# Where and when the turned query weights are loaded, and the weight folding one feed-forward tile earlier, in a two-layer decoder

## The reference

```
h   = sigmoid(xq @ Wg) * (xq @ Wu)      # xq: x rounded to 8 bits by row, W: ternary
x   = layernorm(x + quant(h) @ Wd)             # feed-forward, d_ff = 1024

c   = x @ Wkvc                                 # latent, 64 wide, shared by all heads
k_h = [c @ Wkdec_g, rope(c @ Wkrope_g)]        # 4 key groups g for 16 heads h
q_h = [x @ Wq_h,    rope(x @ Wqrope_h)]
x   = layernorm(x + softmax(causal(q k^T)) v @ Wo),   v = c @ Wvdec_g
```

## Time and profile before

| what | value |
|---|---|
| median of 3 runs (lowest to highest) | 765.69 us (765.66 to 766.63) |
| the profiled execution: its time | 770.09 us |
| its span | 767.6 us |
| mean granted TensorE clock | 0.942 |
| TensorE busy, of the span | 654.6 us, 85% |
| VectorE, ScalarE, GpSimd busy | 63%, 57%, 26% |
| moved by DMA | 62.02 MB, mean 81 GB/s |

### The profile page before, as it was taken

How to read it: one execution, slowest core, us unless ns; L and a number is a source line. 1 busy time by engine, 2 the same in 40 slices (tenths; PEclk the granted TensorE clock), 3 DMA queues, 4 the chain that set the end, 5 groups by cost and what they waited for, 6 DMA issues and landing times.

```text
span 767.6 us, 13772 instructions
## 1 busy us (share of the span) xinstructions
PE 654.6 (85%) x4748; PEld 531.9 (69%) x4749; DVE 483.6 (63%) x1091; ACT 436.3 (57%) x1123; POOL 201.2 (26%) x364
## 2 busy tenths in 40 slices
PE   6788787998999998878978999999986299999950
PEld 4566577998988988843545677777776178778840
DVE  1577776577586577475845656566557567777735
ACT  3988846457456456446866646464523256566622
POOL 2455510040010010011213334252326402223224
PEclk9999999999999999987999999999999589999985
DMA  8995000220220220043020000000078211111114
GB/s 303 378 321 165 1 1 1 86 87 1 88 86 1 86 87 1 1 194 81 1 83 1 1 1 3 1 1 2 1 304 327 68 30 48 48 55 48 48 46 145
DMA packets 31921, 62.02 MB, mean 81 GB/s; under 512 B 2452, under 2 KB 26776, under 8 KB 29624
## 3 DMA queue, kind: packets, MB, share of 16 engines
q1 hardware_dynamic: 29848, 56.04, 21.7%
q0 software_dynamic: 2016, 5.22, 1.9%
HBM read 45.80 MB, written 15.55 MB: 80 GB/s over the span
## 4 chain that ended last, share of the span: by engine, by line
PE 57%; ACT 19%; DVE 15%; issue 4%; POOL 3%; DMA 2%; SPq 0%; POOLq 0%; ACTq 0%; DVEq 0%
PE banks L1726 34%; PE bank L1726 23%; ACT arena L742 5%; DVE U_split L1205 4%; ACT arena L1010 4%; ACT U_split L761 2%; DVE mx L1159 1%; DVE dmx L1487 1%; ACT arena L1017 1%; POOL rstd L550 1%; POOL xs L646 1%; DMA ys<-arena 1%; ACT arena L780 1%; DVE arena L1444 1%; DVE bmx L1224 1%
## 5 line engine op out<-in xcount | busy, mean ns | idle before, releaser
L1726 PE MATMUL banks<-U_split 128*128 128x512 f32 (+1 forms) x616 | 147.8, 352 | 4.7 <-DVE U_split L1205 1.9
L1726 PE MATMUL bank<-U_split 128*128 128x256 f32 (+1 forms) x864 | 115.6, 290 | 15.3 <-DVE U_split L1205 15.2
L1726 PEld LDWEIGHTS bank<-U_split 128*128 128x128 f32 x864 | 108.6, 194 | 19.6 <-issue 15.0
L1726 PEld LDWEIGHTS banks<-U_split 128*128 128x128 f32 x616 | 97.0, 190 | 26.6 <-issue 11.6
L761 ACT ACTIVATE U_split<-arena 128x1024 fp32r (+6 forms) x122 | 97.2, 821 | 14.0 <-issue 5.3
L1726 PE MATMUL banks<-cst,arena 128*128 128x128 f32 (+1 forms) x594 | 83.7, 277 | 14.0 <-DMA arena<-xs 11.1
L1726 PE MATMUL banks<-arena 128*128 (+4 forms) x632 | 84.8, 382 | 8.3 <-ACT arena L1010 5.0
L547 POOL TENSOR_SCALAR rstd<-mv 128x1 f32<-128x1 f32 x48 | 11.8, 245 | 301.4 <-DVE mv L1137 269.5
L1726 PEld LDWEIGHTS banks<-cst,arena 128*128 128x128 f32 (+1 forms) x594 | 68.7, 142 | 24.0 <-issue 13.6
L1010 ACT ACTIVATE arena<-banks,dmx 128x128 f32<-128x128 f32 (+1 forms) x128 | 52.1, 419 | 53.8 <-DVE dmx L1487 53.8
L623 POOL TENSOR_SCALAR arena<-arena,dri 128x128 f32<-128x128 f32 (+1 forms) x128 | 52.6, 429 | 91.9 <-DVE dri L1455 91.9
(11 more groups left out here) (225 smaller groups left out, 1161.6 us busy)
## 6 DMA issues: line engine op xcount, KB each, us to landing
arena<-in_w_exp SPq DMA_DIRECT2D x8, 1536.0 KB, 14.3
xs<-arena SPq DMA_DIRECT2D x8, 1032.0 KB, 14.1
arena<-in_ctxT SPq DMA_DIRECT2D x4, 1601.0 KB, 7.2
arena<-in_ctx SPq DMA_DIRECT2D x4, 1536.0 KB
arena<-in_w_f SPq DMA_DIRECT2D x3, 1024.0 KB, 11.6
arena<-xs SPq DMA_DIRECT2D x23, 129.0 KB, 2.0
w_x<-in_w_x SPq DMA_DIRECT2D x9, 256.0 KB, 7.3
arena<-in_w_oh SPq DMA_DIRECT2D x1, 2048.0 KB, 8.1
```

What stands on the lines that cost most here:

```text
L1726: return nc.tensor.matmul(o, w, x, start=start, stop=stop, **k)
```

## The change

- `w_qT` is cut in two (heads 0 to 11 at the start of `ctxT[LO]`'s place, heads 12 to 15 at the start of `ctxT[HI]`'s), `w_qrT` in three (heads 0 to 7 behind the second part of `w_qT`, heads 8 to 11 and 12 to 15 in the places of the row images). `w_qe`, `w_mapT`, `w_vo` and `w_vh` move.
- SyncE loads both parts of `w_qT` and the first of `w_qrT` after the last scores and the last key products, ahead of its wait for `w_oh`'s place. The other two parts are loaded where all was loaded before; they have a semaphore of their own, waited for ahead of `d_fold(4)`. `d_fold(0)` now counts four loads.
- `d_fold(0)` moves from step 2 of the tile loop, behind `f_gate_up(3)`, to step 1, ahead of `f_hiddenT(0)`. Every later fold and turn-back moves up one tile. The last step has no fold, and the turn-back of pair 7 stands at its head, no longer behind `d_query(0)`. ScalarE's order follows.

The matmuls and their operands are the same.

```diff
+        CUT_Q, CUT_R = 12, (8, 12)
+        w_qT_0 = U1.cut(CUT_Q, E)
...
+        w_qT_1 = U1.cut(H1 - CUT_Q, E)
+        w_qrT_0 = U1.cut(CUT_R[0], E)[0:RD, :, :]
...
+            sp.wait_ge(G["b_s"], 4 * TPB * B)
+            sp.wait_ge(G["x_k"], CP * B)
+            load(w_qT_0, d["w_qT"][:, 0:CUT_Q, :], "ld_wqo")
+            load(w_qT_1, d["w_qT"][:, CUT_Q:H1, :], "ld_wqo")
+            load(w_qrT_0, d["w_qrT"][:, 0:CUT_R[0], :], "ld_wqo")
             sp.wait_ge(G["w_tern"], 3)
             load(w_oh, d["w_oh"], "ld_wqo")
             sp.wait_ge(G["b_o"], 2 * B)
-            load(w_qT, d["w_qT"], "ld_wqo")
-            load(w_qrT, d["w_qrT"], "ld_wqo")
+            load(w_qrT_1, d["w_qrT"][:, CUT_R[0]:CUT_R[1], :], "ld_wqr")
+            load(w_qrT_2, d["w_qrT"][:, CUT_R[1]:H1, :], "ld_wqr")
...
 def d_fold(t):
-                    pe.wait_ge(G["ld_wqo"], 48)
+                    pe.wait_ge(G["ld_wqo"], 64)
...
+                if 2 * t == CUT_R[0]:
+                    pe.wait_ge(G["ld_wqr"], 32)
...
 for t in range(NT + 1):
-                if t >= 3:
-                    d_turn_back(t - 3 if t < NT else t - 2)
+                if t >= 2:
+                    d_turn_back(t - 2 if t < NT else t - 1)
+                if t == 1:
+                    d_fold(0)
                 if t > 0:
                     f_hiddenT(t - 1)
                 if t + 1 < NT:
                     f_gate_up(t + 1)
-                if t > 1:
-                    d_fold(t - 2 if t < NT else t - 1)
+                if 1 < t < NT:
+                    d_fold(t - 1)
                 if t > 0:
                     f_down(t - 1)
                 if t == NT - 1:
-                    d_turn_back(t - 2)
+                    d_turn_back(t - 1)
...
                 if t == NT - 1:
-                    d_fold(t - 1)
+                    d_fold(t)
...
             d_query(0)
-            d_turn_back(NT - 1)
             d_latent(0)
```

More of the change, by code:

```diff
@@ L237, in build, with w_qT, w_qrT @@
         zeros = U1.cut(E + 2)
+        CUT_Q, CUT_R = 12, (8, 12)
         U1.start(0)
+        w_qT_0 = U1.cut(CUT_Q, E)
+        U1.start(CT_W)
         w_qe = U1.cut(KT, H1, LAT)
+        w_mapT = U1.cut(E)
+        w_qrT_1 = U1.cut(CUT_R[1] - CUT_R[0], E)[0:RD, :, :]
+        assert U1.at <= SLOT
+        U1.start(SLOT)
+        w_qT_1 = U1.cut(H1 - CUT_Q, E)
+        w_qrT_0 = U1.cut(CUT_R[0], E)[0:RD, :, :]
+        assert U1.at <= SLOT + CT_W
+        U1.start(SLOT + CT_W)
         w_vo = U1.cut(PAIRS, E)
[L241 to L244, removed]
+        w_qrT_2 = U1.cut(H1 - CUT_R[1], E)[0:RD, :, :]
+        U1.start(0)
         w_vh = U1.cut(PAIRS, E)
+        def w_qT(h):
+            return w_qT_0[:, h, :] if h < CUT_Q else w_qT_1[:, h - CUT_Q, :]
+        def w_qrT(h):
+            if h < CUT_R[0]:
+                return w_qrT_0[:, h, :]
+            return w_qrT_1[:, h - CUT_R[0], :] if h < CUT_R[1] else w_qrT_2[:, h - CUT_R[1], :]
         w_f32 = U2.cut(3, 2 * FF)
@@ L353, in build @@
         eri = sb("eri", [P, TPB, KT * HT])
-        names = """ld_x ld_q0 ld_k0 ld_v0 ld_rows ld_x01 ld_ctxT ld_ctxR ld_ffn_lat ld_cbias ld_wqo ld_out
+        names = """ld_x ld_q0 ld_k0 ld_v0 ld_rows ld_x01 ld_ctxT ld_ctxR ld_ffn_lat ld_cbias ld_wqo ld_wqr ld_out
             const_set ln_var ln_rstd ln_done xT_raw xT_done
@@ L928, in _ @@
             for t in range(NT + 1):
-                if t >= 3:
-                    d_turned_back(t - 3 if t < NT else t - 2)
+                if t >= 2:
+                    d_turned_back(t - 2 if t < NT else t - 1)
+                if t == 1:
+                    d_folded(0)
                 if t > 0:
@@ L951, in _ @@
                     d_split_w(1)
-                if t > 1:
-                    d_folded(t - 2 if t < NT else t - 1)
+                if 1 < t < NT:
+                    d_folded(t - 1)
                 if t == NT - 1:
-                    d_turned_back(t - 2)
+                    d_turned_back(t - 1)
                 if t % TPB == 0 and t // TPB + 1 < B:
@@ L960, in _ @@
                 if t == NT - 1:
-                    d_folded(t - 1)
-            d_turned_back(NT - 1)
+                    d_folded(t)
             d_latent(0)
@@ L2135, in d_fold @@
                 for i in range(2):
-                    mm(half(i, 0), w_kd[:, g, :], w_qT[:, 2 * t + i, :], stop=False)
+                    mm(half(i, 0), w_kd[:, g, :], w_qT(2 * t + i), stop=False)
                 for i in range(2):
-                    mm(half(i, 0), k_turn[:, 2 * t + i, :], w_qrT[:, 2 * t + i, :], start=False)
+                    mm(half(i, 0), k_turn[:, 2 * t + i, :], w_qrT(2 * t + i), start=False)
                 for i in range(2):
```

## The result

The changed kernel takes 773.81 us (median of four runs, 769.81 to 776.51) against 765.74 for the kernel before (four runs): a ratio of 1.0091, 95% interval 1.0054 to 1.0129. Run again with many more runs of both, it is 1.0057, 1.0032 to 1.0082. The forecast was 763.6 us with a range up to 767.0. The change makes the kernel slower, by 0.6 to 0.9%.

What follows compares the result with a forecast made beforehand. TensorE, with 57% of the chain, bounds the kernel; a 2.15 us stall before `d_fold(0)` and the low clock behind it were the target. 1.2 us at tile 3 plus 0.9 in the tail, off 765.69: 763.6 us, range 762.0 to 767.0.

Steps and rivals of the forecast that it cites:

- Early loads: `w_qT` and first `w_qrT` part, issued after the last scores, land by 324 and cost nothing; `w_oh` still issued at 335.07.
- The fold doesn't fill the gap: TensorE's 3.92 us gap before `f_hiddenT(0)`: `d_fold(0)` still waits for `w_oh`, landing at 343.2 after 8.1 us (7.5 to 9.5).
- `w_oh` lands sooner: Rival, chance 0.11: without the loads behind it `w_oh` lands near 342.0, the fold mostly fills the gap; 762.3 us.
- Cost at the start: `d_fold(0)` at low clock delays `f_hiddenT(0)` by 3.8 us; with 1.0 to 1.3 regained in `f_gate_up(2)`, tile 1 comes 2.8 late.
- the clock comes back late: Rival, chance 0.26: the rise at 347.9 moves behind `f_gate_up(2)`, 1.4 us more, 765.0 us, no visible change.
- What comes back: Between tiles 2 and 3, 4.27 us of stall and low-clock work vanish; less 2.8 and 0.3, tile 3 comes 1.2 us earlier.
- the sum: Whole kernel: 1.2 us from tile 3 plus 0.9 in the tail, 2.1 us gained, taken off the median 765.69: 763.6 us.
- The tail: After tile 7, `d_latent(0)` follows `d_query(0)` at once, without a turn-back between: 0.9 us gained.
- slower rival: Rival, chance 0.15: a clock fall behind the wait before `f_down(6)` costs up to 3.4 us, 767.0; 0.11 ends slower.
- the rest moves as a block: Behind the feed-forward stage, from the latent attention on, all shifts together and changes no length.
- The level: Profiled execution 770.09 us, median 765.69, 4.4 us lower; the gain was taken off the median though its clock history may differ.
- the fall behind the stall: TensorE around `d_fold(0)`: a 2.15 us stall near 352, followed by 6.8 us at half clock, 354.7 to 361.5.

Runs made afterwards that it cites:

- c_after: The changed kernel again, unchanged, in the same batch as c_before: 773.18 us, ratio 1.0057 to the kernel before.
- e1: The changed kernel's early loads and new places, with folds and turn-backs in the order of the kernel before: 767.35 us, ratio 0.9991 to the kernel before.
- e7: The changed kernel with the two late `w_qrT` loads issued only after `w_oh` has landed: ratio 1.0055 to the kernel before.
- e9: The changed kernel with first fold behind `f_gate_up(2)`, late `w_qrT` loads after `w_oh`'s landing, idle matmuls in the tail's waits: 765.09 us, ratio 0.9948 to before.
- e10: e9 without the idle matmuls in the tail: ratio 0.9988 to the kernel before.
- c_before: The kernel before again, unchanged: 768.07 us, ratio 1.0011.
- c_before2: The kernel before once more, unchanged, one profiled execution: 761.26 us.
- e8: The changed kernel with 27 idle matmuls in three waits of the feed-forward stage's tail: ratio 1.0023 to the kernel before.
- e2: The changed kernel with the first fold behind `f_gate_up(2)`, not ahead of `f_hiddenT(0)`: 767.37 us, ratio 0.9988 to the kernel before.
- e6: The changed kernel with 40 idle matmuls ahead of `d_fold(0)` while TensorE waits for `w_oh`: 770.78 us, ratio 1.0041 to the kernel before.
- e4: The changed kernel whose first fold multiplies query weights in place of `w_oh`, so doesn't wait for it: 769.55 us, ratio 1.0005 to the kernel before.

## Why the prediction was wrong

**Early loads: right.** Issued at 310, landed in time, `w_oh` issued as before (335.15 in c_after, 335.07 in the earlier trace rows). e1 shows that nothing is lost by them.

**The fold doesn't fill the gap: right, and mis-sized.** It waited for `w_oh` and ran at the low clock with groups 1.05 us apart. But the landing took 8.8 and 9.5 us; I took 8.1, the row of before, and 9.5 was my upper end. With two small loads onto 64 partitions behind it, `w_oh` takes longer (8.7 to 10.3 us in the kernels that have them there, 7.7 to 8.1 before, 8.2, 7.9 and 8.1 in e7, e9 and e10). In these three nothing is queued behind it, in the kernel before two large loads are, and the landing is the same: my rival "`w_oh` lands sooner" had the wrong premise. The Trainium skill's fit ("DMA: Bandwidth & Descriptors", "Anatomy of one DMA") gave 6.8; no landing of `w_oh` here is that short.

**"Cost at the start", 2.8 us: it was 4.1 and 5.2 to 5.4.** Of the excess 0.7 to 1.4 us is the landing. The rest is the clock: I gave back 1.0 to 1.3 us because `f_gate_up(2)` would fall behind the rise at 347.9. Counted from the issue of `w_oh` that is 12.8 us; the rise came at 14.7 in the profile shown of after, amid these matmuls, and at 16.1 in c_after, behind nearly all of them. 0.4 and 0.1 us came back. That was my rival "the clock comes back late": it came in half in one profile, in full in the other.

**"What comes back", 4.27 us: the step that failed.** I read the 9.91 us between tiles 2 and 3 of before as a property of the kernel. It differs from execution to execution. Without the fall, seen in c_before and c_before2, the distance is 6.8 and 6.2 us, and the kernel after has 5.9: 0.3 to 0.9 us come back, not 4.0. Against the one profile that I had read, the term did come out, at 4.0; there the 5.8 us that the forecast missed are 1.3 at the start, 3.4 in the tail and 1.1 behind it. But the sum was taken off the median of other, faster runs. From tile 3 to tile 7 both take 22.2 to 22.3 us, so the shift is kept, as forecast; only it is +3.6 to +4.6 us and not -1.2.

**The tail, -0.9 us: not seen.** `d_latent(0)` did follow `d_query(0)` at once, and the gain went into the clock: tile 7 to the first score takes 15.3 and 13.8 us, where before has 12.8, 14.3 and 14.0. This is the mechanism of my slower rival, and its place was right: behind the wait of 1.96 us ahead of `f_down(6)`. A second wait, 1.12 us ahead of the last `f_down`, is new: `d_fold(7)` had stood there, and I had costed its leaving at nothing, "as the queries wait for VectorE". A step that hides nothing may still keep the clock up: in all nine profiles of the new order of folds without idle matmuls in the tail the clock is low behind this wait or the next, ahead of `d_query(0)`, in none of the five of the old order (e1 is the fifth) and in neither of e8 and e9, where the waits are filled. But against the usual 14.0 to 14.3 us of before it explains 1.2 us of the loss in one profile and nothing in the other, not the 3.4 that I gave the rival; for c_before and c_before2 have the same fall behind the wait ahead of `f_down(6)` (mean 0.56 over 384 to 386 in c_before). A chance of 0.11 for slower was too small chiefly since the loss had a cause that I had not listed: the gain was not there to be had.

**Behind the stage: +0.9 us**, 369.2 against 368.1 to 368.4, where I had said that the rest moves as a block. Every kernel with the new places takes 161.4 to 161.6 us from the first score to the load of the second expert, the old ones 161.0 to 161.2. Why these 0.3 us, and where the other 0.6 come from, no run settles; the low stretch of e2's router is in neither profile of after.

**The sum again**, against the mean of c_before and c_before2: in the profile shown of after +4.2 at tile 1, -0.6 at tile 3, +1.1 in the tail, +0.9 behind, 5.6 us; in c_after +5.3, -0.6, -0.4, +0.9, 5.2 us. The medians differ by 5.7 in the batch of c_after. With the profile shown of before in the mean, the two of after are 4.8 us longer. In the first comparison the four runs of before lay within 1 us of each other, at 765.7; the next batch has a median of 767.5 and runs up to 775.05. Four close runs are no proof of a narrow spread.

**The level.** I took the profiled execution's 2.1 us off the median of the other runs and said that its clock history might differ, and then priced nothing for that. That sentence should have been the main rival: "the fall behind the stall is in some executions only", worth 3.6 us at tile 7 and by itself enough to turn the sign.

## What to carry to other kernels

A low clock behind a stall seen in one profile is not the stall's price: ask what the step costs with and without the fall, and make the case without it a rival of its own. A step moved into a gap pays only if its last operand is there before the gap ends; here the fold waited past it, and one place further back (e2) it cost nothing. And a wait of 1 to 2 us on the critical path of a busy TensorE can be worth filling with idle matmuls: 27 of them brought some 0.4% here (e9 against e10, whose intervals just overlap), 0.3% on top of the changed kernel (e8, overlapping too), and 19 nothing that can be told in the kernel before. Where they left 1.66 us of the wait (e6), the clock fell behind it.

## What the runs showed of the hardware

- The same kernel falls to the low clock at different places in different executions, with the same waits. The wait of 1.97 us ahead of `f_down(6)` was followed by no fall in the profile shown of before and by one at 384.2 in c_before, where the wait is the same 1.97; low stretches of this stage lasted from 3.4 us (343.3 to 346.7 in c_before) over 10.2 (341.0 to 351.2 in c_after) to 13.6 (384.0 to 397.7 in e4). The runs of c_before spread from 764.4 to 775.8 us with mean clocks from 0.951 down to 0.932. The Trainium skill ("TensorE: Matmul & The Clock Gate", "Part 1: The HAM clock gate") says that the number of matmuls at the low clock at the start of a kernel differs from run to run; the traces show such a difference all along the kernel, and the amount is larger than what I wanted to measure.
- Two loads of 256 KB onto 64 partitions, queued behind a transfer, slow it: 2048 KB in 8.7 to 10.3 us with them, 7.9 to 8.2 with nothing behind it. With 2048 KB and 1024 KB behind it, as in the kernel before, it is 7.7 to 8.1 us, so it is not any load behind that does it; what it is about the small ones was not tested.
- Waits of 1.66 us were followed by a fall (e6, at 344.7), waits of 1.62 were not (c_before, 353.9). From the length of a wait alone it can't be told here.
